# A graph layer and eight experts on one Trainium2 core: the last stage's reciprocal root computed on VectorE, and its two expert weights from one Tanh

## The reference

```python
N, F = 12500, 256                      # nodes, features; 212500 edges sorted by dst
h  = layernorm(x)                      # (x - m) / sqrt(v + 1e-5), per row
s  = h @ W1
z  = segment_sum(edge_weight[:, None] * s[src], dst) + s
z  = relu(batchnorm(z) * gamma + beta) @ W2
x1 = x + segment_sum(edge_weight[:, None] * z[src], dst) + z
t  = layernorm(x1)
p  = softmax(t @ router_w.T)           # 8 experts
w, e = top_k(p, 2); w = w / max(w.sum(-1), 1e-12)
o  = t
for k in range(8):
    o = o + combine[:, k] * (gelu(t @ w1[k] + b1[k]) @ w2[k] + b2[k])   # exact gelu
out = x1 + o
```

## Time and profile before

| what | value |
|---|---|
| median of 3 runs | 4628.79 us (4623.98 to 4629.16) |
| the profiled execution's own time | 4638.37 us |
| its span | 4636.6 us |
| PE busy | 3811.2 us, 82% of the span |
| DVE busy | 3319.8 us, 72% |
| ACT busy | 3034.7 us, 65% |
| POOL busy | 2864.8 us, 62% |
| mean granted clock of PE | 0.937 |

### The profile page before, as it was taken

One profiled execution on the slowest core, in us unless ns is written; L12 is line 12 of the kernel. 1 busy time (PEld: TensorE's weight loads), 2 busy tenths in 40 slices (PEclk: granted clock), 3 DMA queues, 4 the chain that ended last, 5 costly groups with the idle time before them and its releaser, 6 DMA issues.

```text
span 4636.6 us, 84123 instructions
## 1 busy us (share of the span) xinstructions
PE 3811.2 (82%) x26914; PEld 3306.3 (71%) x26914; DVE 3319.8 (72%) x8731; ACT 3034.7 (65%) x6515; POOL 2864.8 (62%) x2961
## 2 busy tenths in 40 slices
PE   1688888888789999955788888888888888888988
PEld 1677877887677777744577777777777777777867
DVE  8788888888688888855466666666666666666655
ACT  3688888888777777753455555655556555555555
POOL 0377776777566666546766666666666666666541
PEclk9999999999899999975799999999999999989989
DMA  8788888887799898863333333333333333333221
GB/s 237 278 313 312 315 310 309 309 311 282 264 316 309 310 311 299 297 188 111 93 99 100 110 101 96 107 100 103 105 102 105 101 100 109 101 98 106 82 75 29
DMA packets 308793, 857.93 MB, mean 185 GB/s; under 512 B 47937, under 2 KB 133018, under 8 KB 305852
## 3 DMA queue, kind: packets, MB, share of 16 engines
q0 software_dynamic: 140032, 442.58, 29.1%
q1 hardware_dynamic: 166148, 396.53, 26.7%
q10 hardware_dynamic: 2172, 13.35, 0.8%
HBM read 545.71 MB, written 306.56 MB: 184 GB/s over the span
## 4 chain that ended last, share of the span: by engine, by line
PE 51%; DVE 15%; ACT 12%; issue 11%; another core or an unknown queue 6%; DMA 4%; POOL 2%; SPq 0%; ACTq 0%; DVEq 0%; POOLq 0%
PE ps L1733 10%; PE ps L1754 8%; PE ps L1624 4%; PE ps L1461 4%; PE ps L891 3%; DMA L<-msgd 3%; PE ps L849 2%; PE ps L1628 2%; PE ps L892 2%; PE ps L860 2%; PE ps L1626 2%; DVE S L1407 2%; PE ps L848 2%; ACT gH L1605 2%
## 5 line engine op out<-in xcount | busy, mean ns | idle before, releaser
L1537 POOL DMA_INDIRECT G<-h,tabT x1440 | 1481.6, 1029 | 809.5 <-issue 385.1
L956 ACT ACTIVATE A<-ps,A 128x256 f32<-128x256 f32 x1728 | 692.0, 514 | 94.0 <-PE ps L892 89.5
L1007 POOL DMA_INDIRECT msgd<-A,tabT x432 | 549.6, 1272 | 291.5 <-ACT A L956 196.5
L1833 ACT ACTIVATE ps<-ps,b1T 128x500 f32<-128x500 f32 (+1 forms) x432 | 267.7, 620 | 697.2 <-remote 381.4
L1605 ACT ACTIVATE gH<-G,tabT 128x256 fp32r<-128x256 f32 x960 | 454.4, 503 | 275.2 <-PE ps L1628 102.6
L1584 DVE SCALAR_TENSOR_TENSOR gL<-G,tabT,gH 128x256 fp32r<-128x256 f32 x960 | 448.9, 481 | 115.8 <-ACT gH L1605 59.8
L1998 DVE SCALAR_TENSOR_TENSOR X<-ps,X 125x256 f32<-125x256 f32 x800 | 347.4, 478 | 248.7 <-remote 200.6
L891 PE MATMUL ps<-winH,DT 128*128 128x256 f32 x1728 | 469.1, 304 | 63.5 <-issue 39.5
L1626 PE MATMUL ps<-gH,s 128*125 128x256 f32 x1067 | 353.0, 332 | 110.2 <-ACT gH L1605 60.1
L892 PE MATMUL ps<-winL,DT 128*128 128x256 f32 x1728 | 433.1, 283 | 0.0
L1628 PE MATMUL ps<-gL,s 128*125 128x256 f32 x1067 | 339.0, 319 | 73.9 <-DVE gL L1584 37.8
(11 more groups left out here) (338 smaller groups left out, 11076.3 us busy)
## 6 DMA issues: line engine op xcount, KB each, us to landing
L<-msgd SPq DMA_DIRECT2D x400, 520.0 KB, 5.7
A<-sbd SPq DMA_DIRECT2D x54, 861.0 KB
msgd<-A SPq DMA_DIRECT2D x100, 325.0 KB
G<-h,tabT POOLq DMA_INDIRECT x1440
winR<-h SPq DMA_DIRECT2D x108, 128.0 KB
A<-in_x SPq DMA_DIRECT2D x10, 1120.0 KB
h<-A ACTq DMA_DIRECT2D x10, 1120.0 KB
acc<-h SPq DMA_DIRECT2D x10, 1120.0 KB
```

Of the source, the lines that this page charges most:

```text
L956: e.activation(M[:, n, 0:F], psum[4 + v % 4][:, (n % 2) * F:(n % 2 + 1) * F], ACT.Identity, scale=M[:, n, F + 2:F + 3]).then_inc(evc, 1)
L1007: e.indirect_dma_start(msgd, bass.IndirectOffsetOnAxis(ap=idxI[g % 4][:, t:t + 1], axis=0), msg[g % 3][:, t * 4 * RW:(t + 1) * 4 * RW], No ...
L1537: e.indirect_dma_start(B.G[c % GRL], None, of, bass.IndirectOffsetOnAxis(ap=tab3[:, m, 0:1].bitcast(I32), axis=0)).then_inc(gatl[c % GRL], 16)
```

## The change

In the norm step the reciprocal root moves to DVE altogether. A first value comes from the bits of the variance (a shift by one and RSQ0 minus the result), and two steps of third order refine it: y = y (1.875 + h (0.375 h - 1.25)) with h = y y var. The Sqrt on ACT, its two semaphores and the reciprocal L1898 go away. ACT keeps its two ticks of that step. The tick that stood behind L1895 on DVE now stands inside the first refinement. In the router step DVE copies the logits, takes the eight largest of them, signals ACT with the difference of the first two, and goes on to the places; ACT computes Tanh of half the difference on n columns in place of Exp on 8n; DVE forms the two weights with two instructions. The order of the ticks on DVE changes: the first now stands behind the places (L1944), the second behind the cast (L1947).

```diff
@@ -67,6 +67,7 @@
 ROWS = {3: 0, 7: 4, 11: 8, 14: 12, 18: 15, 21: 19, NS - 1: 22}
 NEXP = 8
 EPS = 1e-05
+RSQ0 = 0x5f3759df
 PR = 8
 RL = 8
 NBB = 3
@@ -403,7 +404,7 @@
         ld_xt = sem("ld_xt")
         st_o = [sem(f"st_o{k}") for k in range(4)]
         ld_ex, wsp = sem("ld_ex"), sem("wsp")
-        d2_tr, d2_cp, d2_z, d2_x1, d2_v, d2_sq, d2_t, d2_o = (sem(n) for n in ("d2_tr", "d2_cp", "d2_z", "d2_x1", "d2_v", "d2_sq", "d2_t", "d2_o"))
+        d2_tr, d2_cp, d2_z, d2_x1, d2_t, d2_o = (sem(n) for n in ("d2_tr", "d2_cp", "d2_z", "d2_x1", "d2_t", "d2_o"))
         d2_tt, d2_tc, tsp, d2_lg, d2_k, rt_s, rt_e, rt_c = (sem(n) for n in ("d2_tt", "d2_tc", "tsp", "d2_lg", "d2_k", "rt_s", "rt_e", "rt_c"))
         d2_ct, d2_cc, d2_b2, d2_o2 = (sem(n) for n in ("d2_ct", "d2_cc", "d2_b2", "d2_o2"))
         l1s, gel, hhi, hlo, l2s, moe = (sem(n) for n in ("l1s", "gel", "hhi", "hlo", "l2s", "moe"))
@@ -1786,8 +1787,6 @@
                 for h in range(0, n, 2):
                     tick()
                 yield
-                e.wait_ge(d2_v, i + 1)
-                e.activation(v[:, 12:12 + n], v[:, 8:8 + n], ACT.Sqrt).then_inc(d2_sq, 1)
                 tick()
                 tick()
                 yield
@@ -1807,9 +1806,8 @@
                 m.then_inc(d2_o, 1)
                 tick()
                 yield
-                p8 = rt[:, 8:8 + 8 * n]
                 e.wait_ge(rt_s, i + 1)
-                e.activation(p8, p8, ACT.Exp).then_inc(rt_e, 1)
+                e.activation(rt[:, 4:4 + n], rt[:, 0:n], ACT.Tanh, scale=0.5).then_inc(rt_e, 1)
                 tick()
                 tick()
                 tick()
@@ -1892,11 +1890,27 @@
                     own.done(e.bn_aggr(v[:, 2 * j:2 * j + 2], stats[:, 6 * j:6 * j + 6]))
                 e.wait_ge(own.s, own.n)
                 v3 = v[:, 0:8].rearrange("p (b k) -> p b k", k=2)
-                e.tensor_scalar(v[:, 8:8 + n], v3[:, 0:n, 1], EPS, None, ALU.add).then_inc(d2_v, 1)
-                tick()
-                e.wait_ge(d2_sq, i + 1)
-                own.done(e.reciprocal(v[:, 16:16 + n], v[:, 12:12 + n]))
+                var, y, h = v[:, 8:8 + n], v[:, 16:16 + n], v[:, 12:12 + n]
+                own.done(e.tensor_scalar(var, v3[:, 0:n, 1], EPS, None, ALU.add))
                 e.wait_ge(own.s, own.n)
+                own.done(e.tensor_single_scalar(h.bitcast(I32), var.bitcast(I32), 1, op=ALU.logical_shift_right))
+                e.wait_ge(own.s, own.n)
+                own.done(e.tensor_scalar(y.bitcast(I32), h.bitcast(I32), -1.0, float(RSQ0), ALU.mult, ALU.add))
+                e.wait_ge(own.s, own.n)
+                for it in range(2):
+                    q_ = rt[:, 240:240 + n]
+                    own.done(e.tensor_tensor(h, y, y, ALU.mult))
+                    e.wait_ge(own.s, own.n)
+                    own.done(e.tensor_tensor(h, h, var, ALU.mult))
+                    e.wait_ge(own.s, own.n)
+                    own.done(e.tensor_scalar(q_, h, 0.375, -1.25, ALU.mult, ALU.add))
+                    e.wait_ge(own.s, own.n)
+                    own.done(e.tensor_tensor(q_, q_, h, ALU.mult))
+                    e.wait_ge(own.s, own.n)
+                    own.done(e.scalar_tensor_tensor(y, q_, 1.875, y, ALU.add, ALU.mult))
+                    if it == 0:
+                        tick()
+                    e.wait_ge(own.s, own.n)
                 e.wait_ge(d2_tr, 2 * (i + 1))
                 for j in range(n):
                     m = e.tensor_scalar(Zs[:, j * F:(j + 1) * F], X[:, j * F:(j + 1) * F], v[:, 2 * j:2 * j + 1], v[:, 16 + j:17 + j],
@@ -1920,43 +1934,29 @@
 
                 def r(at, w=1):
                     return rt[:, at:at + n * w] if w == 1 else rt[:, at:at + n * w].rearrange("p (b e) -> p b e", e=w)
-
-                def wide(a):
-                    return a.rearrange("p (b o) -> p b o", o=1).broadcast_to([R, n, 8])
                 p8, m8 = r(8, 8), r(48, 8)
                 ix, ixf = rt[:, 88:88 + 8 * n].bitcast(U32), r(128, 8)
                 e.wait_ge(d2_lg, i + 1)
-                own.done(e.tensor_reduce(r(0), L, AX.X, ALU.max))
-                e.wait_ge(own.s, own.n)
-                e.tensor_tensor(p8, L, wide(r(0)), ALU.subtract).then_inc(rt_s, 1)
-                tick()
-                e.wait_ge(rt_e, i + 1)
-                own.done(e.tensor_reduce(r(0), p8, AX.X, ALU.add))
-                e.wait_ge(own.s, own.n)
-                own.done(e.reciprocal(r(4), r(0)))
-                e.wait_ge(own.s, own.n)
-                own.done(e.tensor_tensor(p8, p8, wide(r(4)), ALU.mult))
+                own.done(e.tensor_copy(p8, L))
                 e.wait_ge(own.s, own.n)
                 for j in range(n):
                     own.done(e.max(m8[:, j, :], p8[:, j, :]))
                 e.wait_ge(own.s, own.n)
+                e.tensor_tensor(r(0), m8[:, :, 0], m8[:, :, 1], ALU.subtract).then_inc(rt_s, 1)
                 for j in range(n):
                     own.done(e.max_index(ix[:, 8 * j:8 * j + 8], m8[:, j, :], p8[:, j, :]))
                 tick()
                 e.wait_ge(own.s, own.n)
                 own.done(e.tensor_copy(rt[:, 128:128 + 8 * n], ix))
-                own.done(e.tensor_tensor(r(0), m8[:, :, 0], m8[:, :, 1], ALU.add))
-                e.wait_ge(own.s, own.n)
-                own.done(e.tensor_scalar(r(0), r(0), 1e-12, None, ALU.max))
-                e.wait_ge(own.s, own.n)
-                own.done(e.reciprocal(r(4), r(0)))
-                e.wait_ge(own.s, own.n)
-                own.done(e.tensor_tensor(m8, m8, wide(r(4)), ALU.mult))
+                tick()
+                e.wait_ge(rt_e, i + 1)
+                own.done(e.tensor_scalar(r(120), r(4), 0.5, 0.5, ALU.mult, ALU.add))
+                own.done(e.tensor_scalar(r(124), r(4), -0.5, 0.5, ALU.mult, ALU.add))
                 e.wait_ge(own.s, own.n)
                 g0, g1 = r(168, 8), r(208, 8)
                 for j in range(n):
-                    own.done(e.tensor_scalar(g0[:, j, :], iota_f[0:R, 0:8], ixf[:, j, 0:1], m8[:, j, 0:1], ALU.is_equal, ALU.mult))
-                    own.done(e.tensor_scalar(g1[:, j, :], iota_f[0:R, 0:8], ixf[:, j, 1:2], m8[:, j, 1:2], ALU.is_equal, ALU.mult))
+                    own.done(e.tensor_scalar(g0[:, j, :], iota_f[0:R, 0:8], ixf[:, j, 0:1], rt[:, 120 + j:121 + j], ALU.is_equal, ALU.mult))
+                    own.done(e.tensor_scalar(g1[:, j, :], iota_f[0:R, 0:8], ixf[:, j, 1:2], rt[:, 124 + j:125 + j], ALU.is_equal, ALU.mult))
                 e.wait_ge(own.s, own.n)
                 e.tensor_tensor(C[:, 0:8 * n].rearrange("p (b e) -> p b e", e=8), g0, g1, ALU.add).then_inc(rt_c, 1)
                 tick()
```

## The result

The changed kernel took **4602.51 us**, the median of 6 runs (4596.58 to 4613.18), against 4628.98 for the kernel before (6 runs, 4623.49 to 4633.22): a ratio of 0.9949 with a 95% interval of 0.9935 to 0.9962, so 24 us faster by the ratio, 26 by the medians. The prediction said 4640.5, slower by 12. The profiled execution took 4601.88 us (span 4600.1, mean granted clock 0.933).

What follows compares the result with a forecast made beforehand. PE was taken to pace the last stage, held at the norm by two gates. Norm +41, router -25.5 and table loads -4 summed to +11.7 us on the 4628.8 median, giving 4640.5; range 4604 to 4672.

Steps and rivals of the forecast that it cites:

- rival (1): Norm step: the delay is absorbed because ACT paces the stretch behind it and enters early; 4599 to 4609 us, chance 0.26.
- Norm step, +41: DVE's longer root chain delays PE, 1.58 or 2.08 us later by kind of superblock; +41 us, bounds 24 and 52.
- both gates: PE's two waits at the norm: for gH then gL of the first tick's chunk, and for DVE's next tick; the second moves 1.58 us.
- a forecast of -29.5: The gain left if the norm step's delay is absorbed whole, giving 4599 us.
- Router step, -25.5: Router step 1.7 us shorter per superblock, counted where PE waits for it; -25.5 us, -37 if all PE idle time went.
- The 15.4 us read from the 12 waits for gL: Behind the router step, 12 of 21 superblocks with a gather have PE waiting at L1628; capped at 1.7 or so each.
- as forecast (8.4): Router gain in superblocks 22 to 26, without a gather, where L1708 waits 1.6 to 3.9 us; 8.4 us.
- Table loads, -4: Loads ahead of Gelu, mostly hidden in waits; removing them gains 4 us, bounds 0 and -18.
- (2): A slower clock: more PE idling drops the clock in further superblocks; 4659 us, or 4678 if half drop; chance 0.10.
- Rival (3): Tanh is not in Gelu's table, so 54 loads remain and the loads' gain is lost; 4644.5 us, chance 0.12.

Runs made afterwards that it cites:

- e5: The changed kernel run again, against the kernel before, with prompt semaphore updates: -3 us [-8, +2].
- D: Group of runs on one chip, late updates: kernel before (4650.67 us), its repeat, the whole change (-12 us), the norm step alone (+6), the router step alone (-17).
- e9: The kernel before, unchanged, run again for a trace of its own, against the kernel before: +2 us [-7, +10].
- e10: The changed kernel run beside its parts, against the kernel before, with late updates: -12 us [-20, -4].
- e12: The kernel before with only the changed router step, repeated beside the whole change, against the kernel before: -17 us [-26, -7].
- e8: The changed kernel plus an unread Sqrt and Exp that bring the table loads back, against the kernel before: -1 us [-6, +4].
- e3: The kernel before with Sqrt replaced by Copy and Exp by Tanh (root and softmax not computed), against the kernel before: -7 us [-14, 0].
- e7: The changed kernel with ScalarE waiting for the variance again, a small Copy where Sqrt stood, against the kernel before: -1 us [-7, +4].
- e15: The changed kernel with ScalarE's variance wait and a small Copy put back, late updates, against the kernel before: -4 us [-10, +1].
- first pair: The first measurement of the changed kernel beside the kernel before, with late updates: 4602.51 us against 4628.98.
- e1: The changed kernel with the old router step, so the norm step alone, against the kernel before: +4 us [-3, +11].
- e11: The norm step alone (old router step kept), repeated beside the whole change, against the kernel before: +6 us [-2, +14].
- e2: The kernel before with only the changed router step, against the kernel before: -15 us [-21, -9].
- e4: The changed kernel with one refinement of the root in place of two, against the kernel before: -12 us [-20, -4].
- e13: The changed kernel run again as a base for three variants, late updates, against the kernel before: -10 us [-19, -1].
- e14: The changed kernel with three refinements in place of two, late updates, against the kernel before: +6 us [-1, +13].
- e17: The changed kernel with one refinement in place of two, prompt updates, against the kernel before: -23 us [-32, -15].
- e6: The changed kernel with three refinements in place of two, prompt updates, against the kernel before: +8 us [+3, +13].
- E: Group of runs on one chip, late updates: kernel before (4648.87 us), the change (-10 us), three refinements (+6), ScalarE's wait restored (-4), a DVE tick moved earlier (-11).
- e18: The changed kernel with two second-order steps of three instructions in place of two of five, prompt updates, against the kernel before: -20 us [-26, -13].
- C: Group of runs on one chip, prompt updates: kernel before (4277.90 us), the change (-3 us), three refinements (+8), ScalarE's wait restored (-1), table loads restored (-1).
- F: Group of runs on one chip, prompt updates: kernel before (4279.24 us), one refinement (-23 us), two shorter second-order steps (-20).
- B: Group of runs on one chip, late updates: kernel before (4655.73 us), norm step alone (+4 us), router step alone (-15), functions swapped (-7), one refinement (-12).

## Why the prediction was wrong

**The step that failed** is the sentence against rival (1): "ACT enters the stretch with a Gelu that waits for PE (3.06 us), so a late PE makes all of it late." The wait is there, but by the ends that the trace gives it is not for PE's work: in the trace of before the product is done 4.62 us ahead of the Gelu in the mean, and at least 1.48 in each of the 21 superblocks. What ends the wait is PE's signal. The superblock that the prediction reads is the one with the least gap of all. The last product that its Gelu at 3082.82 needs:

```profile
3080.31 1.04 PE L1733 MATMUL ps<-t1L,w1H 128*128 128x500 f32 x2
```

It ends at 3081.35. With the longer chain the product comes 2.07 us later and the Gelu 0.63 earlier: the delay is taken out of the gap. A wait in these rows names the engine that signals and not the time at which its work ended, and I read the one for the other. The Gelu's start laid beside the end of its last L1733 would have shown it; that is the view I left out.

**Norm step, +41.** Its local part held: 2.99 us to the first normalised row in the superblock shown and 2.89 in the mean (3.03 forecast), 1.68 us more idle time for PE at the norm (1.58 forecast), both gates where they were said to be. What was multiplied by 22 was not: alone the step cost 4 and 6 us where updates are late, outside the bounds of 24 to 52. Where they are prompt a chain is paid for in the main, 15 us for each us. The norm step alone was not run there; an estimate by that slope is 1.66 x 15 = 25 us, inside the bounds, which would leave -28 for the rest of e5's -3, against a forecast of -29.5.

**Router step, -25.5.** The step itself is as priced, 3.62 us against 3.7. Alone it gave 15 and 17 us, loads of Exp included. Its end comes 1.4 us earlier in the full superblocks of D (33.35 in e9, 31.90 in e10), but the b2 product on PE does not move (48.02 in e9, 48.12 in e10). The 15.4 us read from the 12 waits for gL (15.1 at the cap of 1.7) are the oversized term. In e12's profiled execution the full superblocks gain nothing against e9's (97.93 to 97.91 us each), and the stretch from the norm of superblock 22 to that of 26 gains 8 (240.3 to 232.3), as forecast (8.4). That is half of the 17 measured; the other half these two traces don't locate.

**Table loads, -4.** e8 puts them back for 1 us by the ratios, e3 takes them away for 7 [0, 14], both within 0 to 18. Rival (3) is refuted: the changed kernel has 2 loads in the stage. The Trainium skill, "ScalarE: Activation LUTs", section "Table sets: the hidden batching unit", lists tanh with other sets and not with gelu's; the trace differs, and it decides.

**The rivals.** (1) is the one that came true, and its 4599 to 4609 hold the result. Its place was right and its mechanism was not: it had ACT entering the stretch early thanks to the load and the wait it is spared, and e7, e8 and e15 put these back for 1 to 6 us. (2) is told below. My test for (1), that the idle time within 8 us of the norm would not grow by 1.5, was a wrong one: it grew by 1.68 and was given back behind those 8 us. So was the one for (2), a clock under 0.93 in the last stage: it is 0.92 there in the trace of before, and 0.91 in the changed one.

**What the clock took.** Rival (2) was at work at the norm itself. In the first 12 us behind the variance the clock is at its lower level in 16 of 21 superblocks before and in all 21 after, for 75 and 136 us together (82 and 136 in e9 and e10). Elsewhere there is less of it, so that between superblocks 1 and 22 the lower level takes 273 and 300 us in the first pair, 321 and 338 in e9 and e10. Every run has its granted clock on record, and the span times what the clock lacks to full is TensorE time lost. Means over the runs, against the kernel before of the same group, good to some 8 us:

| kernel | time | lost to the clock |
|---|---|---|
| norm alone, e1; e11 | +4; +6 | +23; +19 |
| router alone, e2; e12 | -15; -17 | -6; -15 |
| one step, late, e4 | -12 | +9 |
| the change, late, e10; e13 | -12; -10 | +6; +15 |
| three steps, late, e14 | +6 | +29 |
| one step, prompt, e17 | -23 | -5 |
| the change, prompt, e5 | -3 | +14 |
| three steps, prompt, e6 | +8 | +32 |

The norm step alone loses some 20 us to the clock and costs 4 and 6, so what was absorbed is more than the delay by itself. And where a refinement is paid, 20, 11 and 16 us, the clock alone takes 18, 18 and 14. Whether it is the delay that is paid or the slower clock that comes with it, no run here separates: none holds the clock and lengthens the chain.

**What stays open.** Why the first pair gained 24 us [-30, -18] and groups D and E 12 [-20, -4] and 10 [-19, -1]; the intervals only just meet. What holds TensorE's updates back in some groups: no kernel was tried that changes it, and nothing in the traces names it. Nor do they tell whether the signal alone is late or the product too: a matmul's start is recorded, its end is modelled. So that the gap pays the chain rests on where the Gelu stands in the traces and on the norm step's +4 and +6 alone; no run changed the lateness by itself. Whether the third refinement's 16 us with late updates is a kink or a slope: the intervals, some 8 us to each side, allow a milder one.

**A version that beats both.** With prompt updates e18 with its shorter chain gave 20 us and e17 23, where the change, in another group, gave 3. With late ones one refinement gave 12, as the change did; e18 was not run there.

## What to carry to other kernels

A delay put into one engine is paid only as far as the next wait that is longer for another reason. Before multiplying it by the number of steps, lay the start of the consumer two stages on beside the end of what it needs, and see what it waits for in between. Where the consumer starts long after the end of what it needs, that slack isn't the kernel's: it can be gone in another group of runs, as in C and F here, and the change that was free may then be paid for. So measure a small gain in more than one session, with the kernel before beside it each time, lay the granted clocks beside the times, keep dependent chains short even where a trace says that they are hidden, and fuse small instructions (e18's four saved ones took 0.8 us of chain).

## What the runs showed of the hardware that was not expected

- One kernel, two speeds: the kernel before took 4278 and 4279 us in two groups and 4629 to 4656 in the others. In the slower groups TensorE's semaphore updates came a median 1.0 to 1.2 us behind its matmuls, those of VectorE and ScalarE 0.01 us behind their instructions (first pair), and PE had waits under "issue" inside product streams; in the faster ones all came within 0.02 us in the median, and there were no such waits. The mean granted clock of the changed kernel was 0.933 (first pair) and 0.953 (e5). Groups C and E were run under the same chip number, and so were B and F, so the number doesn't say which of the two it will be. The clock is the smaller part: between superblocks 1 and 22 the first pair's changed kernel takes 225 us more than e5 and has 147 us more at half clock, 73 us of TensorE time.
- Tanh and Gelu need no table load between them (2 loads in the stage in place of 106).
- A chain of dependent instructions on four columns runs at 0.20 us from start to start (3063.19, 3063.39, 3063.59 in the norm step shown), on integers too: the 0.32 there (3062.47 to 3062.79) is an exception, the median of the 27 such steps being 0.205.
